# Six rounds of a transformer pipeline: the third window's scores move ahead of the last attention's query on TensorE, and ScalarE's and VectorE's orders follow

## The chip, the cores and the metric

The kernel runs on one core of one Trainium2 chip. The metric is the device time of one execution in microseconds (us). Five engines take part, each with an instruction stream of its own that runs strictly in the order written: TensorE (PE in the profile), VectorE (DVE), ScalarE (ACT), GpSimd (POOL) and SyncE (SP), which issues all DMAs. They meet only through semaphores.

## The reference

The input x is 4 batches of 1024 tokens with 256 channels. Two layers follow each other. Layer 0 is a transformer block with modulated norms, layer 1 is a cross attention with a modulated norm. Cut to what matters:

```python
def layer0(x, mod, context):                      # modulations from silu(mod) @ w_ada
    h = ln(x) * (1 + sc_msa) + sh_msa
    # roll by 64 tokens, windows of 128, 16 heads of 16 channels, softmax(q k / 4) v, roll back
    x = x + (window_attention(h) @ w_so + b_so) * g_msa
    h = ln(x) * (1 + sc_mca) + sh_mca
    # 64 context tokens: scores, top_k(16), softmax over those 16, weighted sum of values
    x = x + (topk_cross_attention(h, context) @ w_co + b_co) * g_mca
    h = ln(x) * (1 + sc_mlp) + sh_mlp
    u = h @ w_m1 + b_m1                           # 256 -> 2048
    x = x + ((silu(u[..., :1024]) * u[..., 1024:]) @ w_m2 + b_m2) * g_mlp
    return x

def layer1(x, x_kv, t):                           # x_kv: the 64 context tokens
    q = ada_ln(x, t) @ Wq + bq                    # "last query" in the kernel
    k, v = split(ada_ln(x_kv, t) @ Wkv + bkv)
    return x + softmax(q k / 4) v @ Wp + bp       # 16 heads of 16, plain softmax over 64 keys
```

All of it is float32.

## The kernel before

**Blocks and rounds.** The 4096 tokens are 8 blocks of 512 tokens, each 4 tiles (windows) of 128. The blocks go through a software pipeline of three stages. After two starting passages (`first`, `second`) come six equal rounds `full(a)` for a = 2 to 7, and then `last`. In round a, block a goes through the window attention, block c = a - 1 through the top-16 search of the cross attention, and block b = a - 2 through the MLP and the last attention. In the trace the rounds a = 4, 5 and 6 lie at about 360 to 469, 469 to 578 and 578 to 688 us. "Even rounds" are those with even a.

**What sets the order.** Nothing is scheduled by a program: the order of each engine is written out by hand in `full` (and in `front_and_middle`), once for each engine. The function `bank_order` is a fourth list: it numbers every PSUM bank filling of the program and deals them out to the 8 banks in turn. A filling may start only when the filling eight places before it in this list has been read out ("drained"); `fill_wait` puts that wait on TensorE. So the list decides which reader holds up which product.

**Names.** `scores_for_max(a, w)` (fillings A, one for each of 4 row groups) are the scores of window w from which VectorE takes the row maxima (`window_max`, `negm<-bank`, L1253). `window(a, w)` is what this text calls a window unit: TensorE turns the maxima (filling mT, L1716), multiplies keys by queries into four banks (B, `q_by_parity,qk`), waits until ScalarE has copied the turned maxima (L864), and subtracts them by 16 more products (`mTs,head_rows`); ScalarE then takes four exponentials out of the banks (L868). The unit that moves is `window(a, 2)`, the third of four. `window_values(a, w)` (PV) multiplies by the values; ScalarE inverts the denominators (`self_denominator`, L857 and L859), VectorE divides (`window_divide`, L1259).

`last_query(b)` is the query of layer 1 (fillings q3: 8 matmuls `hT,w_last`, copied out by ScalarE in two pieces, L833). `last_for_max(b, u)` (A3, `kbd,qk`, 4 banks for each of the halves u = 0 and 1) are its scores, and `last_max` takes their maxima by eight VectorE reductions (L1324). `last_scores`, `last_exps`, `values(4, b)` and `project(4, b)` follow. `project(1, a)` is the output product of the window attention (`w_so,oT_self`).

`topk(c, t, steps)` is the top-16 search on VectorE for tile t: step 0 takes the best eight of each head (16 MAX8), step 1 removes them (16 replacements, L1297), step 2 takes the next eight, step 3 removes them, step 4 sums and masks (L1286 to L1289). `gated_linear(b, j)` (L1316) reads the two MLP fillings of hidden chunk j (ua, ub) out of their banks; `silu(b, j)` on ScalarE (L920) waits for `gated_linear(b, j - 2)`. `take_values` (L1244) reads the values of block a out of a bank; `input_rest` (L1309, two instructions) makes the low part `h_low` of the MLP input, which TensorE needs at the end of the first chunk's products.

**The list around the change** (in the round's order, of which each engine takes its part):

```python
yield from by_row_group("A", a, 3)
yield ("PV", a, 1)
yield from by_chunk("q3", b)
yield from window(a, 2)
yield from by_row_group("A3", b, 0)
yield from by_row_group("A3", b, 1)
yield from window(a, 3)
yield ("PV", a, 2)
```

Counted back by eight: the four B fillings of `window(a, 2)` are what A3 of half 1 waits for; the four B fillings of `window(a, 3)` wait for the last three fillings of A3, half 0, and the first of half 1.

Of the kernel before, what the change touches and what calls it, by code (L numbers as in the profile page):

```python
# [54 lines left out]
def bank_order():  # L55
# [6 lines left out]
    def by_chunk(*key):  # L62
        for k in range(KC):
            yield (*key, k)

    def window(n, w):
        yield ("mT", n, w)
        yield from by_row_group("B", n, w)
# [112 lines left out]
    def full(a):  # L181
        b = a - 2
        yield from front_and_middle(a)
        yield from mlp_in(b)
        yield from by_row_group("A", a, 0)
        yield from by_row_group("A", a, 1)
        yield from project(3, b)
        yield from window(a, 0)
        yield from by_row_group("A", a, 2)
        yield from window(a, 1)  # L190
        yield ("PV", a, 0)
        yield from by_chunk("T", 4, b)
        yield from by_row_group("A", a, 3)
        yield ("PV", a, 1)
        yield from by_chunk("q3", b)
        yield from window(a, 2)
        yield from by_row_group("A3", b, 0)
        yield from by_row_group("A3", b, 1)
        yield from window(a, 3)
        yield ("PV", a, 2)  # L200
        yield from by_row_group("B3", b, 0)
        yield ("mT3", b)
        yield from by_row_group("B3", b, 1)
        yield ("PV", a, 3)
        yield from values(4, b)
        yield from project(1, a)
        yield from project(4, b)
# [71 lines left out]
def build(nc, t_in, out):  # L279
    ctx = ExitStack()  # L280
    with ctx:
# [520 lines left out]
        def _(act):  # L802
# [230 lines left out]
            def full(a):  # L1033
                c, b = a - 1, a - 2
                if a > 2:
                    take_probs(b)
                    act.wait_ge(s_cur_middle, 16 * (c // BLKS + 1))
                    modulated(2, c)
                    take_cross(b)
                    query(c)  # L1040
                    front_in(a)
                    take_scores(c)
                    project_qk(a)
                    modulated_and_rounded(b)
                    topk_exp(c, 0)
                else:
                    take_probs(b, (W - 1,))
                    take_scores(c)
                    take_cross(b)
                    front_in(a)  # L1050
                    project_qk(a)
                    topk_exp(c, 0)
                    modulated_and_rounded(b)
                for j in range(J):
                    silu(b, j)
                    if j == 4:
                        exp_tables()
                        topk_exp(c, 1)
                exp_tables()
                topk_exp(c, 2)  # L1060
                window(a, 0)
                window(a, 1)
                self_denominator(a, 0)
                modulated(4, b)
                self_denominator(a, 1)
                last_query(b)
                window(a, 2)
                window(a, 3)
                self_denominator(a, 2)
                last_exps(b)  # L1070
                topk_exp(c, 3)
                self_denominator(a, 3)
                cross_denominator(4, b)
# [89 lines left out]
        def _(dve):  # L1163
# [141 lines left out]
            def input_rest(n):  # L1305

                for k in range(KC):
                    drained_wait(dve, ("T", 3, n, k))
                    nc.vector.tensor_tensor(h_low[:, k, :], h3T[:, k, :], qr[:, k, :], ALU.subtract).then_inc(s_h_low, 1)  # L1309
# [150 lines left out]
            def full(a):  # L1460
                c, b = a - 1, a - 2
                if a == 2:
# [4 lines left out]
                    topk(c, 0, (2,))  # L1467
                    normalise(3, b, (1, a))
                    topk(c, 0, (3, 4,))
                    input_rest(b)  # L1470
                    take_values(a, 0)
                    take_values(a, 1)
                    topk(c, 1, (0,))
                    gated_linear(b, 0)
# [5 lines left out]
                    topk(c, 1, (3,))  # L1480
                    gated_linear(b, 4)
                    topk(c, 1, (4,))
                    gated_linear(b, 5)
                    topk(c, 2, (0,))
                    gated_linear(b, 6)
                    gated_linear(b, 7)
                    window_max(a, 0)
                    window_max(a, 1)
                    topk(c, 2, (1, 2,))
                    residual_moments(3, b, (0,))  # L1490
                    topk(c, 2, (3, 4,))
                    residual_moments(3, b, (1,))
                    window_max(a, 2)
                    normalise(4, b, (3, b))
                    topk(c, 3, (0,))
                    window_divide(a, 0)
                    topk(c, 3, (1,))
                    window_max(a, 3)
                    window_divide(a, 1)
                    topk(c, 3, (2,))  # L1500
                    last_max(b, (0,))
                    last_max(b, (1,))
                    topk(c, 3, (3,))
                    window_divide(a, 2)
                    window_divide(a, 3)
                    topk(c, 3, (4,))
                    cross_divide(4, b, (0,))
                    cross_divide(4, b, (1,))
                    residual_moments(1, a, (0,))
# [4 lines left out]
                else:  # L1514
# [3 lines left out]
                    residual_moments(2, b, (1,))  # L1518
                    normalise(3, b, (1, a))
                    topk(c, 0, (0, 1, 2,))  # L1520
                    input_rest(b)
                    topk(c, 0, (3,))
                    take_values(a, 0)
                    gated_linear(b, 0)
                    topk(c, 0, (4,))
                    take_values(a, 1)
                    gated_linear(b, 1)
                    topk(c, 1, (0,))
                    gated_linear(b, 2)
                    topk(c, 1, (1, 2,))  # L1530
                    gated_linear(b, 3)
                    topk(c, 1, (3,))
                    gated_linear(b, 4)
                    gated_linear(b, 5)
                    gated_linear(b, 6)
# [1 line left out]
                    window_max(a, 0)  # L1537
                    topk(c, 1, (4,))
                    topk(c, 2, (0, 1, 2,))
                    window_max(a, 1)  # L1540
                    residual_moments(3, b, (0,))
                    residual_moments(3, b, (1,))
                    window_max(a, 2)
                    normalise(4, b, (3, b))
                    topk(c, 2, (3,))
                    window_divide(a, 0)
                    window_max(a, 3)
                    window_divide(a, 1)
                    topk(c, 2, (4,))
                    topk(c, 3, (0,))  # L1550
                    last_max(b, (0,))
                    last_max(b, (1,))
                    topk(c, 3, (1,))
                    window_divide(a, 2)
                    topk(c, 3, (2, 3,))
                    window_divide(a, 3)
                    topk(c, 3, (4,))
                    cross_divide(4, b, (0,))
# [86 lines left out]
        def _(pe):  # L1645
# [431 lines left out]
            def full(a):  # L2077
# [12 lines left out]
                transposed(4, b)  # L2090
                scores_for_max(a, 3)
                window_values(a, 1)
                last_query(b)
                window(a, 2)
                last_for_max(b, 0)
                last_for_max(b, 1)
                window(a, 3)
# [157 lines left out]
```

## Time and profile before

| what | us |
|---|---|
| three runs | 966.14, 971.43, 980.86 (median 971.43) |
| the profiled execution, its time | 967.75 |
| the same, first to last instruction (span) | 965.9 |
| PE busy / DVE busy / ACT busy / POOL busy in it | 875.2 / 763.0 / 473.5 / 306.8 |
| mean granted TensorE clock | 0.982 |

The span is what the trace shows; 1.85 us of the execution's time lie around it. Engines' busy times overlap each other. "Busy" of PE includes pipelined matmuls, so 91% is no measure of how well it is used, but a moment in which PE is idle is a wait that can be read.

### The profile page before, as it was taken

What the parts mean: (1) busy time and instruction counts of PE and PEld (TensorE: products, weight loads), DVE (VectorE), ACT (ScalarE), POOL (GpSimd) and SP (SyncE); (2) the same over time, 40 slices, a digit from 0 to 9 for tenths busy, and PEclk for the clock granted to TensorE, in tenths of its full rate; (3) what the DMA queues carried; (4) which work ended last, traced back from release to release, by engine and by line L of the source; (5) the groups of instructions that cost most, each with busy time, mean ns of one, the idle gap of its engine ahead of it and who ended that gap; (6) DMA issues with size and microseconds to landing.
All of it is one profiled execution on the core that took longest, in us unless ns stands there. A gap on an engine that the chain in (4) does not pass through costs nothing.

```text
span 965.9 us, 22093 instructions
## 1 busy us (share of the span) xinstructions
PE 875.2 (91%) x8032; PEld 645.4 (67%) x8032; DVE 763.0 (79%) x4000; ACT 473.5 (49%) x791; POOL 306.8 (32%) x233
## 2 busy tenths in 40 slices
PE   5978879998999899998999899998999986988997
PEld 3756655785778666885678665885678754764774
DVE  3669899996589985999589985999589985996323
ACT  3357536435463556536573556535563454524314
POOL 1215636311162333422162332422152242331101
PEclk9999899999999999999999999999999999899999
DMA  8304011000100102000100102000100101000000
GB/s 311 103 23 170 2 34 52 12 2 2 45 17 1 57 10 75 12 2 3 44 17 2 56 2 84 12 1 2 45 18 1 57 2 34 1 1 1 22 1 22
DMA packets 28651, 32.81 MB, mean 34 GB/s; under 512 B 4176, under 2 KB 25600, under 8 KB 28288
## 3 DMA queue, kind: packets, MB, share of 16 engines
q1 hardware_dynamic: 28544, 31.41, 10.2%
q8 instruction: 64, 1.05, 0.4%
q14 instruction: 43, 0.35, 0.1%
HBM read 25.05 MB, written 6.36 MB: 33 GB/s over the span
## 4 chain that ended last, share of the span: by engine, by line
PE 66%; DVE 22%; ACT 5%; issue 3%; DMA 2%; SPq 1%; POOL 1%; ACTq 0%; POOLq 0%
PE bank L1647 62%; DVE left L1297 6%; DVE top L1295 3%; DVE negm L1324 3%; PE bank L1665 2%; DVE negm L1253 2%; PE bank L1850 2%; ACT arena L868 2%; DVE arena L1316 1%; DVE stats L1169 1%; DVE h_low L1309 1%; SPq L486 1%; DVE x L1227 1%; DVE xh L1181 1%; DMA xin<-in_x 1%
## 5 line engine op out<-in xcount | busy, mean ns | idle before, releaser
L703 POOL TENSOR_TENSOR arena<-arena,topk_sum 128x1024 f32<-128x1024 f32 x32 | 61.3, 1917 | 209.4 <-DVE arena L1289 209.4
L1647 PE MATMUL bank<-w_m,arena 128*128 128x256 f32 x512 | 112.6, 381 | 2.4 <-issue 2.4
L1647 PEld LDWEIGHTS bank<-w_m,arena 128*128 128x128 f32 x512 | 96.6, 190 | 16.8 <-issue 3.2
L1297 DVE MATCH_REPLACE8 left<-top,arena 128x64 f32<-128x64 f32 x512 | 100.0, 225 | 0.0
L1297 DVE MATCH_REPLACE8 left<-top,left 128x64 f32<-128x64 f32 x512 | 100.0, 222 | 0.0
L1253 DVE TENSOR_REDUCE negm<-bank 128x4 f32<-128x512 f32 x128 | 79.4, 692 | 12.8 <-PE bank L1647 12.7
L868 ACT ACTIVATE arena<-bank 128x512 f32<-128x512 f32 x128 | 66.1, 603 | 45.6 <-PE bank L1647 45.6
L920 ACT ACTIVATE rden<-bank,chan 128x512 f32<-128x512 f32 x64 | 44.1, 689 | 87.9 <-PE bank L1647 85.5
L881 ACT ACTIVATE exps<-exps 128x1280 f32<-128x1280 f32 x32 | 40.8, 1276 | 92.5 <-POOL exps L697 92.2
L1647 PE MATMUL bank<-qr,w_m 128*128 128x512 f32 x256 | 83.4, 406 | 0.2 <-ACT qr L824 0.2
L1647 PE MATMUL bank<-qr,m_low 128*128 128x512 f32 x256 | 81.7, 400 | 0.0
L1295 DVE MAX8 top<-arena 128x8 f32<-128x64 f32 x512 | 67.7, 216 | 15.9 <-ACT arena L888 15.9
L692 POOL TENSOR_TENSOR exps<-arena,top 128x1024 f32<-128x1024 f32 x32 | 61.9, 1935 | 36.2 <-DVE top L1295 35.5
L1647 PE MATMUL bank<-h_low,w_m 128*128 128x512 f32 x256 | 70.9, 398 | 2.4 <-DVE h_low L1309 2.4
L1295 DVE MAX8 top<-left 128x8 f32<-128x64 f32 x512 | 68.1, 225 | 0.6
L650 POOL TENSOR_SCALAR veps<-mv 128x4 f32<-128x4 f32 (+1 forms) x32 | 7.5, 235 | 192.2 <-DVE mv L1176 185.5
L1316 DVE SCALAR_TENSOR_TENSOR arena<-bank,chan,rden 128x512 f32<-128x512 f32 x64 | 47.6, 755 | 21.4 <-ACT rden L920 20.8
L897 ACT ACTIVATE arena<-bank 128x512 f32<-128x512 f32 x64 | 32.5, 623 | 59.6 <-PE bank L1850 59.6
L1647 PEld LDWEIGHTS bank<-h_low,w_m 128*128 128x128 f32 x256 | 48.3, 190 | 15.1 <-DVE h_low L1309 3.6
L1647 PE MATMUL bank<-hT,w_qkv 128*128 128x512 f32 x128 | 57.9, 606 | 0.2 <-ACT hT L814 0.2
L1227 DVE TENSOR_TENSOR x<-bank,x 128x512 f32<-128x512 f32 x50 | 34.4, 689 | 29.9 <-PE bank L1647 29.5
L1647 PEld LDWEIGHTS bank<-qr,w_m 128*128 128x128 f32 x256 | 48.9, 191 | 12.5 <-issue 0.5
(164 smaller groups left out, 1897.8 us busy)
## 6 DMA issues: line engine op xcount, KB each, us to landing
w_m<-in_w_m SPq DMA_DIRECT2D x4, 1024.0 KB, 5.6
xin<-in_x SPq DMA_DIRECT2D x4, 512.0 KB, 4.0
arena<-in_w_m SPq DMA_DIRECT2D x1, 2048.0 KB, 8.7
out<-x SPq DMA_DIRECT2D x4, 512.0 KB, 3.5
arena<-in_w_ada SPq DMA_DIRECT2D x1, 1536.0 KB, 11.1
gate<-gate_rows SPq DMA_DIRECT2D x12, 128.0 KB, 3.4
gated_bias<-gate_rows SPq DMA_DIRECT2D x12, 128.0 KB, 3.6
xin<-in_x SPq DMA_DIRECT2D x3, 384.0 KB, 4.2
```

Source lines behind the costliest of these rows:

```text
L692: nc.gpsimd.tensor_tensor(eS, S[:, t, :].rearrange("p (h n) -> p h n", h=H), top[:, :, 0:1].to_broadcast([P, H, LC]), ALU.subtract).then_i ...
L703: nc.gpsimd.tensor_tensor(Sh, Sh, topk_sum[:].unsqueeze(2).to_broadcast([P, H, LC]), ALU.mult).then_inc(s_prob, 1)
L868: drain(nc.scalar.activation(pT_self[:, w % 2, 4 * r:4 * r + 4, :], ps(key).rearrange("p (h q) -> p h q", h=4), ACT.Exp, scale=SCORE_SCALE ...
L881: nc.scalar.activation(exps[:], exps[:], ACT.Exp, scale=SCORE_SCALE).then_inc(s_exp, 1)
L897: drain(nc.scalar.activation(pT[:, 4 * k:4 * k + 4, t * P:(t + 1) * P], ps(key).rearrange("p (h q) -> p h q", h=4), ACT.Copy), key)
L920: drain(nc.scalar.activation(sa[:, j % 2, :], ps(key), ACT.Silu, bias=chan[:, CB["m1"] + j:CB["m1"] + j + 1]), key)
L1227: drain(nc.vector.tensor_tensor(x[:, slot, tiles], ps(key).rearrange("p (t n) -> p t n", t=2), src, ALU.add), key)
L1253: drain(nc.vector.tensor_reduce(negm[:, w, r, 0:4], ps(key).rearrange("p (h n) -> p h n", h=4), AX_X, ALU.max, negate=True), key)
L1295: i = nc.vector.max(eight, scores)
L1297: i = nc.vector.match_replace(left[:, h, :], eight, scores, REPLACED)
L1316: drain(nc.vector.scalar_tensor_tensor(hid[:, j, :], ps(key), chan[:, at:at + 1], sa[:, j % 2, :], ALU.add, ALU.mult), key)
L1647: return nc.tensor.matmul(dst, lhsT, rhs, start=start, stop=stop)
```

## The change

In all six rounds the third window unit (`window(a, 2)`: the turned maxima, the scores and their exponentials) stands ahead of `last_query(b)` on TensorE and on ScalarE and in the list of bank fillings. VectorE's order in the rounds is rearranged at many places: `take_values(a, 0)` stands ahead of `input_rest(b)`; steps of the top-16 search stand elsewhere among the MLP's `gated_linear`; `window_divide(a, 1)` stands behind the first step of the fourth search instead of ahead of the third's end (rounds 3 to 7); and behind `last_max` comes `window_divide(a, 2)` at once instead of a search step. No instruction is added or removed. Nothing changes in `first`, `second`, `last`, on GpSimd or on SyncE.

```diff
@@ bank_order, full
         yield ("PV", a, 1)
+        yield from window(a, 2)
         yield from by_chunk("q3", b)
-        yield from window(a, 2)
         yield from by_row_group("A3", b, 0)
@@ ScalarE, full
                 self_denominator(a, 1)
+                window(a, 2)
                 last_query(b)
-                window(a, 2)
                 window(a, 3)
@@ VectorE, full, rounds 3 to 7 (round 2 alike, with other places of the search steps)
                     topk(c, 0, (0, 1, 2,))
+                    take_values(a, 0)
                     input_rest(b)
-                    topk(c, 0, (3,))
-                    take_values(a, 0)
+                    topk(c, 0, (3, 4,))
+                    take_values(a, 1)
+                    topk(c, 1, (0,))
                     gated_linear(b, 0)
-                    topk(c, 0, (4,))
-                    take_values(a, 1)
+                    topk(c, 1, (1,))
                     gated_linear(b, 1)
-                    topk(c, 1, (0,))
                     gated_linear(b, 2)
-                    topk(c, 1, (1, 2,))
                     gated_linear(b, 3)
-                    topk(c, 1, (3,))
+                    topk(c, 1, (2, 3,))
                     gated_linear(b, 4)
...
+                    residual_moments(3, b, (0,))
                     window_max(a, 1)
-                    residual_moments(3, b, (0,))
...
                     window_max(a, 3)
-                    window_divide(a, 1)
                     topk(c, 2, (4,))
                     topk(c, 3, (0,))
+                    window_divide(a, 1)
                     last_max(b, (0,))
                     last_max(b, (1,))
-                    topk(c, 3, (1,))
                     window_divide(a, 2)
-                    topk(c, 3, (2, 3,))
+                    topk(c, 3, (1, 2, 3,))
                     window_divide(a, 3)
                     topk(c, 3, (4,))
@@ TensorE, full
                 window_values(a, 1)
+                window(a, 2)
                 last_query(b)
-                window(a, 2)
                 last_for_max(b, 0)
```

TensorE, round 5, from the fourth window's score products to the scores of the last window unit. `hT,w_last` is the last query, `kbd,qk` the scores A3 (both halves), the groups `ident,negm` / `q_by_parity,qk` / `mTs,head_rows` are one window unit each. Before:

```order
L1647 MATMUL bank<-qk,q_by_parity 128x128 x16
L1647 MATMUL bank<-arena,vpad 32x128 x16
L1647 MATMUL bank<-arena,ones_half 32x256 x8
L1647 MATMUL bank<-hT,w_last 128x512 x4
L1716 MATMUL bank<-ident,negm 128x128
L1647 MATMUL bank<-q_by_parity,qk 128x256 x8
L1647 MATMUL bank<-mTs,head_rows 128x128 x16
L1647 MATMUL bank<-kbd,qk 128x128 x32
L1716 MATMUL bank<-ident,negm 128x128
L1647 MATMUL bank<-q_by_parity,qk 128x256 x8
```

The same place now:

```order
L1643 MATMUL bank<-qk,q_by_parity 128x128 x16
L1643 MATMUL bank<-arena,vpad 32x128 x16
L1643 MATMUL bank<-arena,ones_half 32x256 x8
L1712 MATMUL bank<-ident,negm 128x128
L1643 MATMUL bank<-q_by_parity,qk 128x256 x8
L1643 MATMUL bank<-mTs,head_rows 128x128 x16
L1643 MATMUL bank<-hT,w_last 128x512 x4
L1643 MATMUL bank<-kbd,qk 128x128 x32
L1712 MATMUL bank<-ident,negm 128x128
L1643 MATMUL bank<-q_by_parity,qk 128x256 x8
```

The last query now stands directly ahead of the products that read it, and the window unit no longer stands between them (line numbers fall by four).

VectorE, rounds 3 to 7, from the fourth window's maxima (the first row) to the step that ends the fourth search. `L1324` is `last_max`, `L1259` is `window_divide`. Before:

```order
L1253 TENSOR_REDUCE negm<-bank 128x4 x4
L1259 TENSOR_TENSOR oT_self<-bank,rden_self 128x2x128
L1286 TENSOR_REDUCE topk_sum<-exps 128x16
L1288 RECIPROCAL topk_sum<-topk_sum 128x16
L1289 SCALAR_TENSOR_TENSOR arena<-left,exps 128x1024
L1295 MAX top<-arena 128x8 x16
L1324 TENSOR_REDUCE negm<-bank 128x2x4 x8
L1297 MATCH_REPLACE left<-top,arena 128x64 x16
L1259 TENSOR_TENSOR oT_self<-bank,rden_self 128x2x128
L1295 MAX top<-left 128x8 x16
L1297 MATCH_REPLACE left<-top,left 128x64 x16
L1259 TENSOR_TENSOR oT_self<-bank,rden_self 128x2x128
```

The same place now:

```order
L1253 TENSOR_REDUCE negm<-bank 128x4 x4
L1286 TENSOR_REDUCE topk_sum<-exps 128x16
L1288 RECIPROCAL topk_sum<-topk_sum 128x16
L1289 SCALAR_TENSOR_TENSOR arena<-left,exps 128x1024
L1295 MAX top<-arena 128x8 x16
L1259 TENSOR_TENSOR oT_self<-bank,rden_self 128x2x128
L1324 TENSOR_REDUCE negm<-bank 128x2x4 x8
L1259 TENSOR_TENSOR oT_self<-bank,rden_self 128x2x128
L1297 MATCH_REPLACE left<-top,arena 128x64 x16
L1295 MAX top<-left 128x8 x16
L1297 MATCH_REPLACE left<-top,left 128x64 x16
L1259 TENSOR_TENSOR oT_self<-bank,rden_self 128x2x128
```

The division of the second window moved behind the search's maxima, and that of the third window moved ahead of the replacements.

## Rows read from the trace of the kernel before

**Rows 1.** Busy time by stretch, round 5: us, PE, PEld, DVE, ACT, POOL, clock, DMA, GB/s.

```profile
468.70:577.80 109.10, 104.37 (x980) 77.50 (x979) 92.73 (x496) 57.41 (x95) 39.83 (x30) 1.00 0.09 27
```

**Rows 2.** TensorE's waits, whole run: us in total, times, longest.

```profile
PE bank L1647 <- ACT arena L868: 14.5, 14, 1.3
```

**Rows 3.** Timeline of TensorE, round 5: start, us, what, [idle before <- releaser].

```profile
547.61 3.70 PE L1647 MATMUL bank<-hT,w_last 128*128 128x512 f32 x8
551.15 0.27 PE L1716 MATMUL bank<-ident,negm 128*128 128x128 f32 x1
...
552.26 0.67 PE L1647 MATMUL bank<-mTs,head_rows 32*128 32x128 f32 x16
552.76 1.11 PE L1647 MATMUL bank<-kbd,qk 32*128 32x128 f32 x32
555.16 1.17 PE L1647 MATMUL bank<-kbd,qk 32*128 32x128 f32 x32 [1.29 <-ACT arena L868]
...
557.16 1.10 PE L1647 MATMUL bank<-q_by_parity,qk 32*128 32x256 f32 x13 [0.56 <-DVE negm L1324]
...
560.50 1.14 PE L1647 MATMUL bank<-qk,kbd 32*128 32x512 f32 x8
...
570.79 3.72 PE L1647 MATMUL bank<-w_so,oT_self 128*128 128x256 f32 x16
```

**Rows 4.** Timeline of ScalarE, round 5.

```profile
548.16 0.42 ACT L859 ACTIVATE rden_self<-rden_self 128x256 f32<-128x256 f32 x1
...
551.35 0.69 ACT L833 ACTIVATE qk<-bank,chan 128x512 f32<-128x512 f32 x1 [0.17 <-PE bank L1647]
551.94 0.27 ACT L864 ACTIVATE mTs<-bank 128x128 fp32r<-128x128 f32 x1
```

**Rows 5.** Timeline of VectorE, round 5.

```profile
553.89 4.91 DVE L1324 TENSOR_REDUCE negm<-bank 128x8 f32<-128x512 f32 x8 [1.14 <-PE bank L1647]
...
561.80 0.44 DVE L1259 TENSOR_TENSOR oT_self<-bank,rden_self 128x256 f32<-128x256 f32 x1
...
569.52 0.42 DVE L1259 TENSOR_TENSOR oT_self<-bank,rden_self 128x256 f32<-128x256 f32 x1 [2.01 <-ACT rden_self L859]
```

**Rows 6.** The page's costliest groups: form xcount | busy us, mean ns of one.

```profile
L1297 DVE MATCH_REPLACE8 left<-top,arena 128x64 f32<-128x64 f32 x512 | 100.0, 225 | 0.0
...
L1295 DVE MAX8 top<-left 128x8 f32<-128x64 f32 x512 | 68.1, 225 | 0.6
```

**Rows 7.** Timeline of TensorE in `last`, around its last query.

```profile
868.42 1.65 PE L1665 MATMUL bank<-ident,xh 128*128 128x128 f32 x8 [2.86 <-DVE xh L1181]
870.50 5.40 PE L1647 MATMUL bank<-hT,w_last 128*128 128x512 f32 x8 [0.43 <-ACT hT L814]
876.72 2.07 PE L1647 MATMUL bank<-kbd,qk 32*128 32x128 f32 x64 [0.82 <-issue]
```

**Rows 8.** Timeline of ScalarE in `last`, the second copy of that query.

```profile
875.93 0.69 ACT L833 ACTIVATE qk<-bank,chan 128x512 f32<-128x512 f32 x1 [0.17 <-PE bank L1647]
```

**Rows 9.** Timeline of TensorE, round 2, last window unit.

```profile
229.10 2.09 PE L1647 MATMUL bank<-q_by_parity,qk 32*128 32x256 f32 x16 [0.57 <-DVE negm L1324]
...
233.99 1.14 PE L1647 MATMUL bank<-qk,kbd 32*128 32x512 f32 x8
```

**Rows 10.** Busy time by stretch, round 2 (columns as in Rows 1).

```profile
229.00:233.00 4.00, 3.90 (x64) 3.60 (x68) 4.00 (x28) 1.07 (x3) 0.00 (x0) 0.57 0.00 0
```

**Rows 11.** Timeline of VectorE, round 6: the two instructions of `input_rest`.

```profile
606.30 2.18 DVE L1309 TENSOR_TENSOR h_low<-xh,qr 128x512 fp32r<-128x512 f32 x1
...
608.41 1.10 DVE L1309 TENSOR_TENSOR h_low<-xh,qr 128x512 fp32r<-128x512 f32 x1
```

**Rows 12.** Timeline of GpSimd, the same moment.

```profile
605.57 2.37 POOL L678 TENSOR_TENSOR x<-x,gated_bias 128x1024 f32<-128x1024 f32 x1
607.88 1.08 POOL L697 TENSOR_TENSOR exps<-top 128x256 f32<-128x256 f32 x1
```

**Rows 13.** Timeline of TensorE, round 6, end of the MLP's first product.

```profile
631.63 1.17 PE L1647 MATMUL bank<-qk,q_by_parity 32*128 32x128 f32 x32 [0.34 <-DVE arena L1316]
```

More of the change, by code:

```diff
@@ L1482, in full @@
                     topk(c, 1, (4,))
+                    topk(c, 2, (0,))
                     gated_linear(b, 5)
-                    topk(c, 2, (0,))
                     gated_linear(b, 6)
@@ L1487, in full @@
                     window_max(a, 0)
+                    topk(c, 2, (1, 2,))
                     window_max(a, 1)
-                    topk(c, 2, (1, 2,))
+                    topk(c, 2, (3, 4,))
                     residual_moments(3, b, (0,))
-                    topk(c, 2, (3, 4,))
                     residual_moments(3, b, (1,))
@@ L1494, in full @@
                     normalise(4, b, (3, b))
-                    topk(c, 3, (0,))
                     window_divide(a, 0)
-                    topk(c, 3, (1,))
                     window_max(a, 3)
+                    topk(c, 3, (0, 1,))
                     window_divide(a, 1)
-                    topk(c, 3, (2,))
                     last_max(b, (0,))
                     last_max(b, (1,))
-                    topk(c, 3, (3,))
+                    topk(c, 3, (2,))
                     window_divide(a, 2)
+                    topk(c, 3, (3, 4,))
                     window_divide(a, 3)
-                    topk(c, 3, (4,))
                     cross_divide(4, b, (0,))
@@ L1520, in full @@
                     topk(c, 0, (0, 1, 2,))
+                    take_values(a, 0)
                     input_rest(b)
-                    topk(c, 0, (3,))
-                    take_values(a, 0)
+                    topk(c, 0, (3, 4,))
+                    take_values(a, 1)
+                    topk(c, 1, (0,))
                     gated_linear(b, 0)
-                    topk(c, 0, (4,))
-                    take_values(a, 1)
+                    topk(c, 1, (1,))
                     gated_linear(b, 1)
-                    topk(c, 1, (0,))
                     gated_linear(b, 2)
-                    topk(c, 1, (1, 2,))
                     gated_linear(b, 3)
-                    topk(c, 1, (3,))
+                    topk(c, 1, (2, 3,))
                     gated_linear(b, 4)
@@ L1547, in full @@
                     window_max(a, 3)
-                    window_divide(a, 1)
                     topk(c, 2, (4,))
                     topk(c, 3, (0,))
+                    window_divide(a, 1)
                     last_max(b, (0,))
                     last_max(b, (1,))
-                    topk(c, 3, (1,))
                     window_divide(a, 2)
-                    topk(c, 3, (2, 3,))
+                    topk(c, 3, (1, 2, 3,))
                     window_divide(a, 3)
```

## The prediction

> **What bounds the kernel now.** I read the busy table of one round first, then the list of who waited for whom on TensorE, then the timelines around the moved unit. In round 5 TensorE is busy 104.4 of 109.1 us at full clock, VectorE 92.7, ScalarE 57.4 [rows 1]. So a round lasts as long as TensorE's work and its waits of under 5 us, and whatever moves a TensorE product later moves the end of the kernel, unless a later wait swallows it. The waits are short and repeat in each round. The largest releaser, ScalarE's exponentials, holds TensorE 14.5 us in 14 waits over the run [rows 2]. One of them in each round is the one that the change is about: between the two halves of A3 TensorE stands 1.29 us because the banks that half 1 fills still hold `window(a, 2)`. Directly behind it the last window unit waits 0.56 us for the maxima of A3 [rows 3].
>
> **Part 1: the query now stands directly ahead of its reader.** Before, the window unit (551.15 to 552.76, 1.61 us) ran while ScalarE copied the query's second piece, and half 0 of A3 began at 552.76 without a wait [rows 3]. Worked out anew from 547.61, where the query began:
> - The window unit takes 1.61 us if nothing holds it. ScalarE, however, still inverts a denominator until 548.16 + 0.42 = 548.58 [rows 4]. Only then does it copy the turned maxima; the products that need them followed that copy's start by 552.26 - 551.94 = 0.32 us [rows 3, 4]. So they begin at 548.90 and the query 0.50 us later (552.76 - 552.26), at 549.40: 0.18 us of new wait.
> - The second copy starts 551.35 - 547.61 = 3.74 us after the query [rows 3, 4], at 553.14.
> - A3 has to wait for that copy. `last` has the same neighbours in this order: copy from 875.93, scores at 876.72, 0.79 us later, and TensorE idle for 0.82 us [rows 7, 8]. A3 half 0 then begins at 553.93, where it began at 552.76: **1.17 us later**.
>
> **Part 2: the 1.29 us wait goes, and what is late next.** The exponentials of the moved unit run under the 3.5 us query, so half 1 of A3 follows half 0 at once. But behind it stands the last window unit, whose banks are freed by `last_max`: three reductions of half 0 and the first of half 1. VectorE started these 553.89 - 552.76 = 1.13 us after half 0 [rows 3, 5], and five of eight reductions are 5/8 of 4.91 = 3.07 us, so the unit can start no sooner than about 4.2 us after half 0 does. It started 557.16 - 552.76 = 4.40 us after it [rows 3]: the 1.29 us wait lay on no path of its own; taken away, it comes back in the next wait. Both halves are issued in 2.07 us in `last` [rows 7], so the unit now waits from about 556.4 to 553.93 + 4.40 = 558.33, 1.9 us where it was 0.56. The unit is 1.17 us late, and so is all behind it. Bounds: 1.0 us if ScalarE's copy is not held up (1.17 less 0.18), 1.4 if the copies collide by another 0.2. I take 1.17, six times: **7.0 us**.
>
> **Part 3: VectorE behind `last_max`.** It now stands ready at 555.06 + 4.91 = 559.97 and has `window_divide(a, 2)` next. Before, that division did not wait at 561.80 [rows 5]; its denominator is 1.17 later, at most 562.97. Then come three search steps in a row: a replacement step is 16 x 100.0/512 = 3.1 us, the maxima 16 x 68.1/512 = 2.1 [rows 6], so 8.3 us, and `window_divide(a, 3)` ends at about 563.4 + 8.3 + 0.4 = 572.1. TensorE's `project(1, a)` wants it at 570.79 + 1.17 = 571.96 [rows 3]. Before there were 2.01 us of slack ahead of that division [rows 5]; they are used up. Bounds 0 to 0.3 a round; I take 0.1: **0.6 us** in six rounds. Of the rest of the rearrangement, `window_divide(a, 1)`, a 0.4 us instruction, ends some 1 us ahead of A3, for which its bank is now needed: nothing.
>
> **Part 4: VectorE in the MLP.** Rounds 3 to 7 have the same set of instructions ahead of the last `gated_linear`, in another order. In even rounds that instruction ends last: TensorE waits 0.34 us for it [rows 13]. Two things pull at it. Three `gated_linear` in a row (1 to 3) run into `silu`, which waits for the second one back: 0.2 us, and up to 0.6 at the last ones. Against that stands `take_values(a, 0)` ahead of `input_rest`. In round 6 the first instruction of `input_rest` took 2.18 us from 606.30 and the second 1.10, and they ended 0.54 and 0.55 us after GpSimd's add and subtraction did (608.48 against 607.94, 609.51 against 608.96) [rows 11, 12]. So they are held until GpSimd is through, and 0.7 us of bank reading ahead of them costs nothing and is saved later. If that reading did add to them, `h_low` would be 0.7 us late in rounds 2, 4 and 6, 2.1 us in all. Value taken: 0, bounds -0.5 to +1.3 in each even round.
>
> The Trainium skill, "SBUF — State Buffer", Terms, has the rule for this: VectorE and GpSimd share one port pair, locked for a whole instruction, and the loser waits. The trace agrees with it: the ends above lie one uncontended instruction behind GpSimd's. By the rule the term is 0, without it 2.1 us.
>
> **Part 5: the clock.** In round 2, the two waits of 1.29 and 0.57 us with the half 1 products between them were followed by a fallen clock: granted 0.57 on the mean from 229 to 233 us, which is 1.2 GHz for most of it, where it is full in round 5 [rows 1, 10]. The distance from the window unit to the next scores was 233.99 - 229.10 = 4.89 us against 560.50 - 557.16 = 3.34 [rows 3, 9]: a fall costs 1.55 us. It happened in one round of six with these waits; a whole wait of 2.86 us in `last` was followed by a slow query of 5.40 against 3.70 us [rows 3, 7]. The new wait of 1.9 us lies between the two, with 0.82 us more ahead of it. I take half of the rounds, two more than before: **3.1 us**; bounds -1.55 (none) and +7.8 (all six).
>
> **Sum.** 7.0 + 0.6 + 0 + 3.1 = 10.7 us. Against the profiled execution's own time of 967.75 that is 978.5; against the median of 971.43 it is 982.1. The three runs spread over 14.7 us, so that either may be the level; I forecast between them, **980**.
>
> **The rivals.**
> - *The bubble is a bank shortage and its removal is worth what it shows.* This one ends on the other side. Its place is the 1.29 us wait; it decides if the last window unit is not held by the five reductions but keeps its own 0.56 us. Then a round gets 1.29 and loses 0.82 + 0.18: -0.3 us, 1.7 in all, and the clock fall of round 2 may go too (-1.55): about 968. For it speaks that the waits' releasers differ; against it the 4.40 us that the reductions explain to 0.2 us.
> The Trainium skill, "Trainium Kernel Development and Optimization", Best Practices, would back this rival: consistent bubbles can mean that SBUF or PSUM has run out. Here the bubble is consistent and on a bank, but the next bank wait is longer by as much.
> - *Swallowed.* The 1.2 us vanishes in a later wait of the round. The even rounds have one for the block's input, but its load stands on SyncE behind the store of the round before, which the same shift delays. Price 0, time 970.
> - *The clock falls in all six rounds*: 967.75 to 971.43 plus 7.6 + 7.8 = 985.
> - *VectorE becomes the bound*: its idle wait ahead of `window_divide(a, 2)` (up to 3 us a round) or the `silu` chain pushes `project(1, a)` or the MLP's end by another 1 us each round: 6 more, 986. For it speaks VectorE's 92.7 of 109.1 us [rows 1]; against it that the slack of 2.01 us [rows 5] is about what the change uses.
>
> **How the numbers follow.** Forecast 0.52 (975 to 984, 980 the likeliest), other side 0.08 (968), swallowed 0.13 (970), clock in all rounds 0.14 (985), VectorE 0.13 (986, up to 991). The range leaves out most of the other-side case and the upper tail: 971 to 989. Two per cent, about what a measurement of this kernel can tell from no change, is 19 us. Faster by more than that no case reaches, 0.02 for a mechanism I don't see; slower by more needs clock and VectorE together or more, 0.07; within it 0.91.
>
> **What would show it.** Right: in each round an idle gap of about 0.8 us between query and A3, none between its halves, 1.6 to 2.0 us ahead of the last window unit, released by L1320 (L1324 before); 4.4 us from A3 half 0 to that unit; a round of 110.3 us and more. Slow products (over 1.5 us where 1.1 is usual) in the last unit of two to four rounds. The forecast is wrong if the last unit starts less than 4 us after A3's half 0, if round 5 is 109 us or less, or if new waits of over 0.5 us stand in the MLP or ahead of `project(1, a)`.

## The result and the profile after

The changed kernel takes 981.58 us (median of 5 runs, 980.35 to 985.5) against 971.43 (5 runs, 966.14 to 980.86): ratio 1.0118, interval 1.008 to 1.0156. The forecast was 980. The profiled execution is the slowest of the five: 985.5 us, span 983.6, mean clock 0.972, against 967.75, 965.9 and 0.982. Of the 46 runs of the kernel before that stand beside the experiments two, of 1062.39 and 991.05 us at clocks of 0.835 and 0.929, are left out of every ratio and of every mean clock given below.

TensorE around the moved unit in round 5, timeline of the kernel after (columns as in [rows 3]); the first row is the second window's unit, `window(a, 1)`, ahead of all that moved:

```profile
547.04 1.10 PE L1643 MATMUL bank<-q_by_parity,qk 32*128 32x256 f32 x13 [1.14 <-ACT arena L868]
...
556.17 3.70 PE L1643 MATMUL bank<-hT,w_last 128*128 128x512 f32 x8
560.70 2.07 PE L1643 MATMUL bank<-kbd,qk 32*128 32x128 f32 x64 [0.82 <-ACT qk L833]
562.69 0.33 PE L1712 MATMUL bank<-ident,negm 128*128 128x128 f32 x1
565.09 1.10 PE L1643 MATMUL bank<-q_by_parity,qk 32*128 32x256 f32 x13 [2.06 <-DVE negm L1324]
...
568.43 1.14 PE L1643 MATMUL bank<-qk,kbd 32*128 32x512 f32 x8
...
578.79 3.69 PE L1643 MATMUL bank<-w_so,oT_self 128*128 128x256 f32 x16
```

The same unit in the kernel before, and the copy that A3 now waits for (timeline of ScalarE, after):

```profile
540.26 1.10 PE L1647 MATMUL bank<-q_by_parity,qk 32*128 32x256 f32 x13 [1.14 <-ACT arena L868]
```

```profile
559.91 0.69 ACT L833 ACTIVATE qk<-bank,chan 128x512 f32<-128x512 f32 x1 [0.17 <-PE bank L1643]
```

Where [rows 3] have one gap of 1.29 us and one of 0.56, there are now 0.82 ahead of A3 and 2.06 behind it. The copy ends at 560.60 and A3 begins 0.10 us later. Both halves of A3 are issued in one piece, and the wait that is gone is in the next one. From A3's first product to the last window unit it is 565.09 - 560.70 = 4.39 us; before, 557.16 - 552.76 = 4.40. A unit that starts 4.4 us after A3 in both orders looks as if it were held by the maxima alone; e3 and e4 below test that. The reductions are in the first row (timeline of VectorE, round 5); five of the eight end at about 561.86 + 5/8 x 4.87 = 564.90, and the unit starts at 565.09:

```profile
561.86 4.87 DVE L1324 TENSOR_REDUCE negm<-bank 128x8 f32<-128x512 f32 x8 [2.55 <-PE bank L1643]
569.44 0.42 DVE L1259 TENSOR_TENSOR oT_self<-bank,rden_self 128x256 f32<-128x256 f32 x1 [2.71 <-ACT rden_self L859]
```

Round 5, from the same point to the same point as [rows 1], at full clock:

```profile
476.34:586.66 110.32, 104.54 (x985) 77.64 (x984) 92.83 (x498) 57.69 (x96) 39.41 (x30) 1.00 0.09 27
```

110.32 - 109.10 = 1.22 us more, with TensorE as busy as before (104.54 and 104.37): the round is longer by waits alone. TensorE's list of waits over the whole run (us in total, times, longest), two lines of before that [rows 2] do not have, then after:

```profile
PE bank L1647 <- DVE negm L1324: 4.8, 8, 0.9
...
PE bank L1647 <- ACT qk L833: 0.8, 1, 0.8
```

```profile
PE bank L1661 <- DVE xh L1181: 14.0, 6, 6.8
PE bank L1643 <- DVE negm L1324: 13.7, 8, 2.1
...
PE bank L1643 <- ACT arena L868: 6.8, 8, 1.1
PE bank L1643 <- ACT qk L833: 5.9, 7, 1.0
```

The exponentials (L868) held TensorE 14 times for 14.5 us [rows 2] and now hold it 8 times for 6.8: 7.7 us gone in six waits. The query's copy (L833) holds it for 5.1 us more and the maxima (L1324) for 8.9: 14.0 us for the 7.7.

The other part of the loss is the clock. Busy time by stretch, after, behind the 2.06 us wait of rounds 2 to 7 (columns as in [rows 1]):

```profile
229.00:236.00 7.00, 6.68 (x92) 4.87 (x92) 4.72 (x26) 2.88 (x7) 0.61 (x1) 0.76 0.01 2
342.00:349.00 7.00, 6.20 (x84) 3.48 (x76) 2.66 (x21) 3.55 (x8) 0.00 (x0) 0.76 0.00 0
453.00:460.00 7.00, 4.94 (x94) 3.33 (x91) 4.29 (x8) 3.04 (x7) 0.00 (x0) 1.00 0.00 0
565.00:572.00 7.00, 5.58 (x96) 3.64 (x96) 4.29 (x28) 3.98 (x9) 0.89 (x1) 1.00 0.01 2
680.00:687.00 7.00, 5.78 (x71) 3.17 (x64) 2.84 (x26) 3.96 (x9) 0.00 (x0) 0.76 0.01 2
790.00:797.00 7.00, 7.00 (x88) 4.86 (x88) 1.48 (x3) 2.73 (x6) 0.64 (x1) 0.54 0.01 2
```

Four of the six rounds have a stretch at 1.2 GHz there, where before had one [rows 10]. In round 7 the unit's products take nearly twice their time (timeline of TensorE):

```profile
789.83 2.09 PE L1643 MATMUL bank<-q_by_parity,qk 32*128 32x256 f32 x16 [2.06 <-DVE negm L1324]
791.32 1.35 PE L1643 MATMUL bank<-mTs,head_rows 32*128 32x128 f32 x16
792.60 1.94 PE L1643 MATMUL bank<-arena,vpad 128*32 128x128 f32 x32
794.30 1.93 PE L1643 MATMUL bank<-arena,ones_half 128*32 128x256 f32 x16
796.17 1.23 PE L1643 MATMUL bank<-qk,kbd 32*128 32x512 f32 x8
```

796.17 - 789.83 = 6.34 us where [rows 3] have 3.34: this fall costs 3.00 us, the one of [rows 9] 1.55.

In the profiled execution the falls behind this wait lengthen the way from the last query to the last attention's scores by 7.9 us in four rounds, where before has its 1.55. A third part lies at the start of rounds 4 and 6, where the block's input comes late and the clock falls too. From `project(1, a)` of an even round to the next query it is 85.3 us in before and 87.0 to 87.3 in after (the moved unit now stands in this stretch); from that of an odd round it is 86.41 and 87.29 in before and 90.18 and 90.89 in after, so 3.8 us more in the two. With 6 x 1.22 these make 7.3 + 6.3 + 3.8 = 17.4 of the 17.7 us between the two spans.

### The profile page after: what moved, and what is told of

The parts are those of the page before. It is cut to its first block, busy times and chain, and to the rows that moved or that the text cites. A ratio compares the mean times of both kernels' runs of the same rounds, so it can differ in the third digit from the quotient of the medians.

```text
span 983.6 us, 22093 instructions
## 1 busy us (share of the span) xinstructions
PE 883.6 (90%) x8032; PEld 650.8 (66%) x8032; DVE 759.7 (77%) x4000; ACT 474.1 (48%) x791; POOL 306.4 (31%) x233
## 3 DMA queue, kind: packets, MB, share of 16 engines
q1 hardware_dynamic: 28544, 31.41, 10.2%
## 4 chain that ended last, share of the span: by engine, by line
PE 73%; DVE 14%; ACT 6%; issue 3%; DMA 2%; SPq 1%; POOL 1%; ACTq 0%; POOLq 0%
PE bank L1643 68%; DVE left L1297 3%; PE bank L1661 2%; DVE negm L1324 2%; DVE top L1295 2%; DVE negm L1253 2%; PE bank L1846 2%; ACT arena L868 2%; SPq L486 1%; DMA xin<-in_x 1%; DVE stats L1169 1%; DVE x L1227 1%; DMA w_m<-in_w_ada 1%; DVE arena L1289 1%; DVE xh L1181 1%
## 5 line engine op out<-in xcount | busy, mean ns | idle before, releaser
L868 ACT ACTIVATE arena<-bank 128x512 f32<-128x512 f32 x128 | 66.1, 603 | 55.2 <-PE bank L1643 55.2
L697 POOL TENSOR_TENSOR exps<-top 128x256 f32<-128x256 f32 x32 | 21.8, 682 | 152.7 <-DVE top L1295 152.7
L1643 PE MATMUL bank<-q_by_parity,qk 32*128 32x256 f32 x512 | 39.0, 420 | 21.3 <-DVE negm L1324 12.4
```

The source lines that it names most:

```text
L697: nc.gpsimd.tensor_tensor(eS_top, top[:], top[:, :, 0:1].to_broadcast([P, H, TOPK]), ALU.subtract).then_inc(s_dif, 1)
L868: drain(nc.scalar.activation(pT_self[:, w % 2, 4 * r:4 * r + 4, :], ps(key).rearrange("p (h q) -> p h q", h=4), ACT.Exp, scale=SCORE_SCALE ...
L1643: return nc.tensor.matmul(dst, lhsT, rhs, start=start, stop=stop)
```

## The experiments

Each was run beside the kernel before on one chip: the first four on one (before: median 968.7 of 23 runs), the last three on another (971.59 of 23). "Window unit 3" is `window(a, 2)`, "unit 4" is `window(a, 3)`. Besides the medians I read one stretch in all of them, round by round: from the start of the last query to the last attention's scores and to `project(1, a)`. A fall of the clock shows in it as 1.4 us or more above the same kernel's other rounds. For before, in rounds without a fall, this stretch is 12.89 us to the scores and 23.18 to `project(1, a)`.

**e1_vector_only: before, with VectorE's new order alone.**

```diff
@@ VectorE's program: that of the changed kernel
@@ TensorE, ScalarE, bank_order: as before
```

> Only VectorE's order is the new one; TensorE, ScalarE and the bank list are those of before. My theory (the loss is the query's exposed copy and the five reductions behind it): TensorE keeps its waits of 1.29, 0.56, 0.69 and 0.76 us in each round, and the time is that of before within 0.3% (969 to 974 us). Rival (VectorE's new order causes a good part of the loss): at least a third of the 10 us, so 975 us or more, with new waits in the MLP or ahead of the window attention's output product.

Measured: 971.5 us (968.46 to 977.4), ratio 1.0021, interval 0.9991 to 1.005. In those of rounds 3 to 7 in which the clock didn't fall, the stretch to `project(1, a)` is 23.26 us, before 23.18: VectorE's new order costs 0.08 us a round. Round 2 is the exception. There `window_divide(a, 1)` now stands behind two search steps, and A3, which takes the bank that it frees, begins 6.53 us after the query, not 5.14. Timelines of VectorE and TensorE:

```profile
228.37 0.41 DVE L1259 TENSOR_TENSOR oT_self<-bank,rden_self 128x256 f32<-128x256 f32 x1
```

```profile
229.02 2.19 PE L1643 MATMUL bank<-kbd,qk 32*128 32x128 f32 x64 [1.22 <-issue]
...
233.41 1.10 PE L1643 MATMUL bank<-q_by_parity,qk 32*128 32x256 f32 x13 [1.94 <-DVE negm L1324]
```

Both halves of A3 then follow at once, and unit 4 starts 233.41 - 229.02 = 4.39 us after them, as ever: its 1.94 us wait is not the cost, the 1.22 us one is. Round 2's stretch to `project(1, a)` is 26.46 us; less the 1.61 of the fall behind it that is 1.7 more than 23.18. So VectorE's order alone costs some 5 x 0.08 + 1.7 = 2.1 us, nearly all in round 2, where the expectation had every wait unchanged. The medians can't tell it from nothing.

**e2_no_vector: the changed kernel with VectorE's old order.**

```diff
@@ VectorE's program: that of the kernel before
@@ TensorE, ScalarE, bank_order: as changed
```

> The opposite half: TensorE, ScalarE and the bank list as changed, VectorE's order as before. My theory: the whole loss stays, 979 to 985 us, with 0.8 us ahead of the last attention's scores and about 2.1 us ahead of the last window unit in each round. Rival: less than two thirds of the loss, 977 us or below.

Measured: 982.76 us (978.32 to 985.55), ratio 1.0143 (1.01 to 1.0186): the whole loss is there, and with 14.1 us rather more than the change's 10.2. Timeline of TensorE in round 5, rows with a wait:

```profile
561.48 2.07 PE L1647 MATMUL bank<-kbd,qk 32*128 32x128 f32 x64 [0.82 <-issue]
565.88 1.10 PE L1647 MATMUL bank<-q_by_parity,qk 32*128 32x256 f32 x13 [2.06 <-DVE negm L1324]
```

The same two gaps as after. (The first is put down to "issue" here and to the copy's L833 after; it is 0.82 us in both.) Round 2 has one of its own, because `window_max(a, 3)` comes too late for the moved unit in the old order:

```profile
221.66 1.10 PE L1647 MATMUL bank<-q_by_parity,qk 32*128 32x256 f32 x13 [2.07 <-DVE negm L1253]
```

VectorE's order does matter there: with the moved unit the old order costs about 2 us in round 2, which the new order saves. It is not where the change's time went.

**e3_unit_between_halves: before, with unit 4 between A3's halves.** If the 1.29 us wait is idle time in which unit 4 could be issued, this is the edit that fills it.

```diff
@@ bank_order and TensorE, full
                 last_for_max(b, 0)
+                window(a, 3)
                 last_for_max(b, 1)
-                window(a, 3)
```

> The kernel before, but the last window unit stands between the two halves of the last attention's scores (TensorE and the bank list), so that its banks wait for one reduction instead of five. If the reductions' chain is what sets the start of that unit: the unit starts about 2.4 us after half 0 instead of 4.4 (then held by the exponentials of the unit before), half 1 ends 0.9 us earlier than the unit did before, and the kernel is about 5 us faster, 964 to 968 us. Rival (the 1.29 us wait on the exponentials is what costs): the wait stays, now ahead of the unit, and the time is that of before.

Measured: 971.48 us (967.87 to 979.25), ratio 1.004 (1.0006 to 1.0074): a miss. Timeline of TensorE in round 5:

```profile
555.39 1.11 PE L1647 MATMUL bank<-kbd,qk 32*128 32x128 f32 x32
...
557.90 1.10 PE L1647 MATMUL bank<-q_by_parity,qk 32*128 32x256 f32 x13 [1.15 <-ACT arena L868]
...
562.25 1.14 PE L1647 MATMUL bank<-qk,kbd 32*128 32x512 f32 x8
...
566.61 1.09 PE L1647 MATMUL bank<-qk,kbd 32*128 32x512 f32 x5 [1.44 <-DVE oT_self L1259]
```

Unit 4 starts 2.51 us after A3, not 4.4, since with half 0 and half 1 apart it no longer stands behind the fifth reduction; and query to last scores falls from 12.89 to 12.00 us, as expected. But the products behind them wait 1.44 us for the bank that `window_divide(a, 2)` frees, behind a search step on VectorE. To `project(1, a)` only 23.18 - 22.97 = 0.21 us are left. The clock fell in three rounds of this profile and in one of before's, and not only there: the mean granted clock of e3's 12 runs is 0.9766, that of 22 runs of before on the same chip 0.9813. Over 972 us a mean clock lower by 0.0047 is 4.6 us of full clock less, so the run can be longer by up to that, against 6 x 0.21 = 1.3 us gained. A wait removed came back one bank later, the second time in this study.

**e4_maxima_twice: before, with four more reductions.** Half 0's four reductions are done twice in the six rounds, the first time into a buffer that nothing reads. If the unit is set by the chain of reductions, every added one moves it.

```diff
@@ VectorE, last_max
                         filled_wait(dve, key)
+                        if u == 0 and n < BLOCKS - 2:
+                            nc.vector.tensor_reduce(extra[:, r],
+                                                    ps(key).rearrange("p (t h n) -> p t h n", t=2, h=4),
+                                                    AX_X, ALU.max, negate=True)
                         drain(nc.vector.tensor_reduce(negm3[:, 2 * u:2 * u + 2, r, 0:4],
```

> The kernel before with each of the four maxima reductions of half 0 of the last attention's scores done twice in the six rounds (the first into a buffer of its own that nothing reads), 2.4 us more work on VectorE in a round. If five reductions set the last window unit's start, it starts 6.8 us after half 0 instead of 4.4, and the kernel is 6 x 2.4 = 14.7 us slower or more (the clock may fall after waits of 3 us, 1.5 us each): 985 to 996 us. Rival (the unit's start is set by the exponentials' wait, the reductions run beside it): the wait grows by less than 1.2 us a round, 972 to 979 us.

Measured: 995.82 us (995.28 to 997.83), ratio 1.0288 (1.0242 to 1.0333), at the range's upper end. Timeline of TensorE in round 7:

```profile
797.02 1.11 PE L1652 MATMUL bank<-kbd,qk 32*128 32x128 f32 x32
799.43 1.17 PE L1652 MATMUL bank<-kbd,qk 32*128 32x128 f32 x32 [1.29 <-ACT arena L869]
...
803.78 2.09 PE L1652 MATMUL bank<-q_by_parity,qk 32*128 32x256 f32 x16 [2.92 <-DVE negm L1329]
```

The unit starts 803.78 - 797.02 = 6.76 us after A3, 2.36 more than before, for four reductions of about 0.6 us: the reductions reach it one for one. The wait of half 1 stays 1.29 us and does not set the unit's start. The clock fell behind the 2.92 us wait in all six rounds; two of them (busy time by stretch):

```profile
461.30:466.30 5.00, 4.93 (x72) 4.30 (x76) 4.82 (x35) 2.07 (x4) 0.00 (x0) 0.50 0.00 0
803.70:808.70 5.00, 4.92 (x71) 4.30 (x75) 4.83 (x35) 2.06 (x4) 0.22 (x1) 0.50 0.01 3
```

At a clock of 0.50, which is 1.2 GHz, for five whole microseconds. Query to last scores at full clock would be 12.89 + 2.36 = 15.25 us; it took 16.85, 17.27, 18.12, 17.60, 18.11 and 17.59, 14.0 more in all. With 6 x 2.36 = 14.2, less the 1.55 that before paid for its own fall, that is 26.7 us. From round 2's query to the end the profile is (996.0 - 222.7) - (965.9 - 219.55) = 27.0 us longer than before's: the account closes. (The medians differ by 27.1; that this fits as well is partly chance, since the median run of before need not have one fall.)

**e5_fourth_unit_ahead: the changed kernel, with unit 4 ahead of A3 too.** It then covers the query's copy, and needs no maxima of A3.

```diff
@@ bank_order and TensorE, full
                 window(a, 2)
                 last_query(b)
+                window(a, 3)
                 last_for_max(b, 0)
                 last_for_max(b, 1)
-                window(a, 3)
```

> The changed kernel, but the fourth window unit too stands ahead of the last attention's scores: units 3, query, unit 4, both halves of the scores. My theory: the query's copy (0.8 us) hides under the fourth unit, whose banks no longer wait for reductions, so both new waits (0.8 and 2.1 us) vanish; what is late next is half 1 of the scores, which waits about 1.3 us for the fourth unit's exponentials. From the last query's block to the scores against the keys the round is 1.7 us shorter than in the changed kernel and 0.5 shorter than before: 965 to 971 us, ratio to before 0.993 to 1.0. Rival (the loss has another cause, since VectorE and ScalarE are as in the changed kernel): it stays at 975 us or more.

Measured: 967.35 us (962.88 to 972.8), ratio 0.9961 (0.9935 to 0.9986): faster than both kernels. Timeline of TensorE in round 5:

```profile
549.50 3.70 PE L1643 MATMUL bank<-hT,w_last 128*128 128x512 f32 x8
553.03 0.27 PE L1712 MATMUL bank<-ident,negm 128*128 128x128 f32 x1
...
554.64 1.11 PE L1643 MATMUL bank<-kbd,qk 32*128 32x128 f32 x32
557.04 1.17 PE L1643 MATMUL bank<-kbd,qk 32*128 32x128 f32 x32 [1.29 <-ACT arena L868]
```

No wait behind the query, none for the maxima, and the 1.29 us wait between the halves is back. From the second window's unit, `window(a, 1)` (540.37), to the last scores (560.02) it is 19.65 us; before 20.24, after 568.43 - 547.04 = 21.39. The kernel with the 1.29 us wait is the quicker one by 1.74 us a round, 10.4 us in six of the 15.3 between this median and that of e7 on the same chip. The mean granted clocks of the two, 0.9802 and 0.9743, leave up to 0.0059 x 975 = 5.8 us to falls, enough for the rest.

**e6_between_and_divide: e3, with `window_divide(a, 2)` directly behind the maxima.** It tests the reading of e3's miss. On top of e3's edit (round 2 alike, ahead of its search step):

```diff
@@ VectorE, full
                     last_max(b, (1,))
-                    topk(c, 3, (1,))
                     window_divide(a, 2)
-                    topk(c, 3, (2, 3,))
+                    topk(c, 3, (1, 2, 3,))
                     window_divide(a, 3)
```

> The kernel before with the fourth unit between the halves of the scores, as in the last set, and with the division of the third window directly behind the maxima instead of behind a search step. There the unit's gain of 0.9 us a round was given back as a wait of 1.44 us for that division where 0.76 stood. Theory: the wait falls back to 0.76, a round without clock falls is 0.9 us shorter than before, and the kernel is 3 to 5 us faster than before if the clock falls as often as before: 963 to 968 us. Rival: something later in the round takes it again, and the time is that of before or above.

Measured: 968.24 us (963.42 to 973.42), ratio 0.9972 (0.9941 to 1.0002). TensorE's row of the wait in question, round 5:

```profile
558.63 1.62 PE L1646 MATMUL bank<-qk,kbd 32*128 32x512 f32 x6 [0.77 <-ACT arena L931]
```

0.77 us on ScalarE, as in before, for the 1.44 on `window_divide`: where e3's gain of 0.9 us a round went is shown. The stretch is 22.36 us in the rounds without a fall (22.30 in round 2), 0.82 less than before. Three rounds had a fall, and the mean clock of the 12 runs is 0.9775 where that of 22 runs of before on this chip is 0.9801: part of the 6 x 0.82 = 4.9 us goes there. The time is just above the range that I expected, and the interval of the ratio just includes no gain.

**e7_changed_again: the changed kernel, without an edit.** The first profile had four falls and long input waits in the even rounds; I wanted to know what of that returns.

```diff
@@ no edit
```

> The changed kernel once more, for a second profile beside the same runs of before. The waits of 0.8 and 2.06 us stand in each round, exactly. What may differ: the number of rounds with a fallen clock behind the 2.06 us wait (3 to 5 of 6 by my theory; 1 if these falls are not tied to the length of the wait) and the waits for the block's input at the start of even rounds (1.16 and 2.17 us in the first profile; 0.3 to 1.4 if those were chance, the same again if the change causes them). Time 978 to 985 us.

Measured: 982.65 us (980.47 to 984.87), ratio 1.0107 (1.0073 to 1.0142). Waits of 0.82 and 2.06 us again, stretch of 22.61 to 22.63 us again, and again four falls, but in rounds 2, 3, 4 and 7 instead of 2, 3, 6 and 7: the waits are fixed, their places of falling are not. On the same chip e5 took 967.35. It differs only in unit 4's place, so the 15.3 us hang on it, falls of the clock included.

## Why the prediction was right

**Part 1** held. From the second window's unit to A3's first product it is 560.70 - 547.04 = 13.66 us, and 552.76 - 540.26 = 12.50 before: 1.16 later, forecast 1.17. The exposed copy is the 0.82 us of `last` [rows 7] in each of rounds 3 to 7. In round 2 the wait is 1.02 us, put down to the copy as well, but by the copy A3 could begin at 224.69. It begins at 224.88, behind `window_divide(a, 1)`, which ends at 224.67 (timelines of VectorE and TensorE, after):

```profile
224.26 0.41 DVE L1259 TENSOR_TENSOR oT_self<-bank,rden_self 128x256 f32<-128x256 f32 x1
```

```profile
224.88 2.07 PE L1643 MATMUL bank<-kbd,qk 32*128 32x128 f32 x64 [1.02 <-ACT qk L833]
```

So the prediction's "nothing" for that division holds in rounds 3 to 7 and is 0.2 us short in round 2.

**Part 2** held, and is the one on which the result turned. The last unit is bound by the reductions: 4.39 us in after, 4.40 in before, 6.76 with four more of them (e4), 2.51 when it doesn't stand behind the fifth (e3). Its wait is 2.06 us where I worked out 1.9, since what TensorE does in between ends 2.32 us after A3's start (562.69 + 0.33) and not at 2.47; the start of the unit was right. Its releaser is L1324, not the L1320 that I gave.

**Part 3** held. Set against the second window's unit (547.04 now, 540.26 before, so 6.78 us to take off), the reductions end at 559.95 (forecast 559.97), `window_divide(a, 2)` waits for its denominator until 562.66, 2.71 us in the row above (562.97 "at most"), and `window_divide(a, 3)` runs from 578.28 for 0.41 us (timeline of VectorE, after), which is an end at 571.9 (572.1), right ahead of `project(1, a)` at 572.01 (571.96). The slack of 2.01 us [rows 5] is gone. The price was 0.08 us a round in e1 alone, and 0.06 in after against e2 (22.62 and 22.56), where I took 0.1. Round 2 pays 0.20 more ahead of `project(1, a)`.

Parts 1 to 3 forecast 7.6 us; measured 6 x 1.22 = 7.3.

**Part 4**, zero, held. Where no fall stands ahead of it, TensorE's wait at the end of the MLP's first product is 0.29 us in an even round (round 4 of e7), 0.34 before [rows 13]; behind a fall it is 0.14 or 0.15 us (rounds 4 and 6 of after, round 6 of e7). Round 5 closes to 1.22 us with nothing left for the MLP. The reason given held too. In round 4 of e7 both instructions of `input_rest` stand behind `take_values` and take 2.54 us where they took 3.20, and their end is still 0.54 us after GpSimd's (393.18 and 392.64). (The shortest of the 16 such instructions of before takes 0.68 us, so the 0.54 us are not quite the one whole instruction of the prediction.) Timelines of VectorE and GpSimd:

```profile
390.64 2.54 DVE L1309 TENSOR_TENSOR h_low<-xh,qr 128x512 fp32r<-128x512 f32 x2
```

```profile
391.55 1.09 POOL L697 TENSOR_TENSOR exps<-top 128x256 f32<-128x256 f32 x1
```

**Part 5** was right in sign, and near in size by a count that is partly chance. I forecast two falls more, three of six rounds; the two profiles of the changed kernel have four of six each, e2 three. The weak step is the base: I took the one fall in six of [rows 10] for what the old waits do. Kernels whose longest wait in this place is mostly 1.1 to 1.4 us (before, e1, e3, e5, e6) have 1, 3, 3, 2 and 3 falls in six rounds, 12 of 30, one of them behind e1's 1.94 us in round 2; e1 differs from before by 0.08 us a round from round 3 on and has two falls there, before none. Behind 2.06 us there are 11 of 18, behind 2.92 us six of six. By these shares the net is 6 x (11/18 - 12/30) = 1.3 falls where I took two, and counts this small would not show even the sign. The mean granted clocks of all the runs do: 0.9807 in 44 runs of before, 0.9750 in 11 of the changed kernel and 0.9763 in e2's six. Over 975 us 0.0057 less is some 11 us more at 1.2 GHz in a run, anywhere in it, so 5.6 us at most.

The price of 1.55 us is the lower end: query to last scores is longer by 1.80, 1.63, 1.47 and 2.99 us in after's four (0.20 of the 1.80 is round 2's division), by 1.6 to 1.8 in e7's, and by 1.6 to 2.9 in e4's. One to three of them at some 1.6 to 2.0 is 2 to 6 us; with 7.3 that holds the 10.2 and 11.1 us between the medians. That the forecast of 980 lies 1.6 us off is luck in part: too many falls at too low a price, and a starting level chosen between two.

**The rivals.** The bank shortage falls by e4 and e5: with the 1.29 us wait back, the kernel is faster. The clock in all rounds is what e4 does and the change doesn't. VectorE as the bound falls by e1, and by what the changed kernel itself shows: from the last scores to `project(1, a)` it is 578.79 - 568.43 = 10.36 us, before 10.29. *Swallowed* falls too: round 5 keeps its 1.22 us, and in the even rounds, where the 1.2 us was to vanish, nothing does. From round 3's query to round 4's it is 446.51 - 332.08 = 114.43 us in after and 109.59 in before, from round 5's to round 6's 113.51 and 110.47. But I passed over the even rounds' input there too quickly. Its load waits behind the store on SyncE, as I said, and TensorE then waited 1.16 and 2.17 us at the start of rounds 4 and 6 in after (0 and 0.85 before), each time with a fallen clock behind it. Before in round 6, and then after, with the stretch behind it:

```profile
592.12 1.65 PE L1665 MATMUL bank<-ident,xh 128*128 128x128 f32 x8 [0.85 <-DVE xh L1181]
```

```profile
601.41 2.21 PE L1661 MATMUL bank<-ident,xh 128*128 128x128 f32 x8 [2.17 <-DVE xh L1181]
```

```profile
601.00:605.00 4.00, 3.59 (x34) 2.85 (x37) 3.93 (x10) 1.55 (x2) 0.00 (x0) 0.60 0.01 2
```

The 2.17 - 0.85 = 1.32 us lie between the store and the input's first use. SyncE issues the store at 578.72 in before and VectorE begins with the new input at 588.29, 9.57 us later; in after it is 586.69 and 597.58, 10.89. Issuing the store's three transfers alone takes 1.57 and 2.55 us (timeline of SyncE, before and after):

```profile
578.72 1.57 SPq L486 DMA_DIRECT2D out<-x  x3
```

```profile
586.69 2.55 SPq L486 DMA_DIRECT2D out<-x  x3
```

It takes 2.46 us in e7 and 2.52 in e1, and 1.57 or 1.58 in e2 to e6, and SyncE's program is the same in all. Whether the change has a part in it stays open: the two waits add up to 3.33 us in after, 2.16 in e7 and 1.32 in e2, and to 0.85, 1.88, 1.98, 0.93 and 1.45 in before, e1, e3, e5 and e6, all from single profiles.

## What to carry to other kernels

Removing a wait on a bank brings its length only if the next wait does not hang on another chain that started earlier: measure from the common start (here A3's first product) to the next unit, and if the operations that free that unit's banks explain the distance, as five reductions did 4.4 us, closing the gap ahead of them gains nothing. Before work is moved from between a product and its reader, look at what it covered: here it hid a 0.82 us copy, and e5, which put another unit in its place, beat both kernels by 0.4% and 1.6%. Count what a clock fall costs from several profiles, not from one, and take how much the clock falls from the mean granted clock of all runs.

## What was not expected of the hardware

The clock fell behind waits that look too short to matter. In e4 a wait of 2.92 us was followed by five microseconds at 1.2 GHz, in which TensorE was 4.9 us busy; behind waits of mostly 1.1 to 1.4 us it fell in 12 of 30 rounds, and in different rounds of the same kernel (after and e7). The length of the longest wait doesn't settle it either: e3 and e6, whose longest in this place are 1.44 and 1.14 us, have mean clocks of 0.9766 and 0.9775, nearer to the changed kernel's 0.9750 than to the 0.9807 of before. Why isn't shown. Three falls more or fewer are some 5 us, where runs of before differ by 13.
